# Attention stages with heads of 8 dimensions: halves of a batch half a slot apart, projections at a slot's end

## What is computed

```python
Q = (x @ Wq.T).reshape(B, xN, NUM_HEADS, HEAD_DIM)        # x: normalised rows
KV = (z @ Wkv.T).reshape(B, zN, 2, NUM_HEADS, HEAD_DIM)   # z: the context, 77 keys
attn = jnp.einsum('bqhd,bkhd->bhqk', Q, K) * SCALE
attn = jax.nn.softmax(attn, axis=-1)
O = jnp.einsum('bhqk,bkhd->bqhd', attn, V).reshape(B, xN, DIM)
return O @ Wo.T
```

## Time and profile before

| what | value |
|---|---|
| median of 3 runs | 6037.49 us (6032.2 to 6039.96) |
| the profiled execution, its own time | 6016.21 us |
| its span, first to last instruction | 6014.5 us |
| granted TensorE clock over the span | 0.916 of full speed |
| PE, PEld, DVE, ACT, POOL busy | 82%, 60%, 65%, 45%, 36% |
| first and last start of `score` in `l0x` | 41.2 and 636.4 us |
| first and last start of `score` in `l2x` | 2583.4 and 3181.3 us |

### The profile page before, as it was taken

One profiled execution on the slowest core, in us unless ns is written; L12 is line 12 of the kernel. 1 busy time (PEld: TensorE's weight loads), 2 busy tenths in 40 slices (PEclk: granted clock), 3 DMA queues, 4 the chain that ended last, 5 costly groups with the idle time before them and its releaser, 6 DMA issues. The chain is left out here.

```text
span 6014.5 us, 133734 instructions
## 1 busy us (share of the span) xinstructions
PE 4935.3 (82%) x41787; PEld 3611.9 (60%) x41787; DVE 3921.6 (65%) x9897; ACT 2728.1 (45%) x5454; POOL 2172.3 (36%) x3095
## 2 busy tenths in 40 slices
PE   6888898999962798078888998888898799998888
PEld 3555466888862465045555665776776577776544
DVE  4555585777766333245555776888887688888544
ACT  3444475555530233044444554555554355554344
POOL 4333100111117100733332334777775733333300
PEclk9999798999985899579997998999999899999988
DMA  1000500000011333100000000000000000000000
GB/s 37 5 4 3 242 0 14 5 5 5 5 49 43 115 135 115 50 10 5 4 3 12 1 0 9 0 0 0 0 0 5 7 2 2 2 2 6 1 11 18
DMA packets 108942, 140.25 MB, mean 23 GB/s; under 512 B 35832, under 2 KB 83256, under 8 KB 103996
## 3 DMA queue, kind: packets, MB, share of 16 engines
q1 hardware_dynamic: 100544, 120.88, 6.0%
q0 software_dynamic: 8192, 16.79, 1.0%
HBM read 47.44 MB, written 58.72 MB: 18 GB/s over the span
## 5 line engine op out<-in xcount | busy, mean ns | idle before, releaser
L2170 POOL TENSOR_TENSOR l3a_probs<-l3a_probs,l3a_later 128x512 f32<-128x512 f32 x256 | 320.7, 1281 | 4.9 <-DVE l3a_total L2358 4.9
L2156 POOL TENSOR_TENSOR l3a_keys<-l3a_kT,head 128x2048 f32<-128x2048 f32 x64 | 230.4, 3600 | 232.8 <-ACT l3a_kT L2283 232.8
L1585 POOL DMA_INDIRECT l1c_rows<-l_rows,l1f_slots x128 | 123.1, 961 | 442.5 <-PEq L1577 402.0
L2218 PE MATMUL l3a_scores<-l3a_keys,l3a_qT 128*128 128x512 f32 x512 | 255.1, 601 | 4.2 <-POOL l3a_keys L2156 4.2
L170 POOL TENSOR_TENSOR l1x_ve<-l1x_mv,eps 128x1 f32<-128x1 f32 x64 | 12.2, 190 | 657.6 <-DVE l1x_mv L162 657.6
L965 DVE SCALAR_TENSOR_TENSOR l0x_p_lo<-l0x_turned,l0x_p_hi 128x512 f16<-128x512 f32 (+1 forms) x192 | 115.7, 603 | 204.4 <-ACT l0x_p_hi L891 202.2
L298 PE MATMUL l3a_po<-l3a_vals,l3a_probsT 128*128 128x32 f32 x2048 | 248.0, 269 | 0.2
L965 DVE SCALAR_TENSOR_TENSOR l2x_p_lo<-l2x_turned,l2x_p_hi 128x512 f16<-128x512 f32 (+1 forms) x192 | 115.7, 603 | 202.8 <-ACT l2x_p_hi L891 200.6
L298 PEld LDWEIGHTS l3a_po<-l3a_vals,l3a_probsT 128*128 128x128 f32 x2048 | 246.8, 192 | 0.7 <-ACT l3a_probsT L279 0.4
L1656 POOL TENSOR_TENSOR l2f_hid<-l2f_prod,l2f_route 128x512 f32<-128x512 f32 x128 | 152.1, 1193 | 257.0 <-DVE l2f_prod L1803 253.7
L254 ACT ACTIVATE l3a_probs<-l3a_probs 128x512 f32<-128x512 f32 x256 | 161.7, 632 | 182.4 <-DVE l3a_probs L245 177.2
(11 more groups left out here) (581 smaller groups left out, 17374.6 us busy)
## 6 DMA issues: line engine op xcount, KB each, us to landing
l_rows<-l0f_zeros SPq DMA_DIRECT2D x34, 1024.0 KB, 26.2
l1f_parts<-l1f_split SPq DMA_DIRECT2D x40, 512.0 KB, 3.6
l1e_x_in<-l_rows SPq DMA_DIRECT2D x40, 256.0 KB, 2.8
l1f_down<-l1f_w SPq DMA_DIRECT2D x40, 256.0 KB, 2.3
l_rows<-l1e_y_out SPq DMA_DIRECT2D x40, 256.0 KB, 2.7
l1f_w<-in_L_W SPq DMA_DIRECT2D x16, 256.0 KB, 3.4
out_x<-x_res SPq DMA_DIRECT2D x16, 256.0 KB, 2.0
x_res<-in_x SPq DMA_DIRECT2D x1, 3840.0 KB, 12.2
```

The lines of the kernel that those rows point to most:

```text
L2156: pool.tensor_tensor(keys[it.par][:, :, :, :], kT[it.par][:, :, :].unsqueeze(2).to_broadcast([P, J, G4, T]), g.head32[:, :].unsqueeze(1).u ...
L2170: pool.tensor_tensor(v, v, later[:, :].unsqueeze(1).to_broadcast([P, 4, T]), ALU.mult).then_inc(s_masked, 1)
L2218: pe.matmul(scores[c][:, 0:G4 * T], qT[it.par][:, c, :], keys[it.par][:, c, :, :].rearrange("p h t -> p (h t)"), start=True, stop=True).th ...
```

## The change

In both stages, the order of all four compute engines is written anew, the softmax halves are set half a slot apart, and the three transposes of a batch are divided over two slots: `turn0` stands in the batch's own slot (`1 if u else 0`), `turn1`, `turn2`, all of `weigh`, `divide`, `turn_o`, `output` and `add` in the slot behind it (`ago` 1 where it was 2 for the last four). Of the front, `x`, `norm`, `rest` (of the context) and `c` move to an earlier turn (lag 0), and PE's `q`, `k`, `v0` and `x` stand at the end of slots 0, 1, 2 and 3, `v1` in the middle of slot 3. A piece's `blank` matmul stays in units 0 and 1 and goes from unit 2 (one of nine). `make_attention_constants` moves from `init` to the start of POOL's list in `l0x`. POOL waits for other counts in `context_rest`.

```diff
@@ pool, l0x and l2x
+                if first_use:
+                    make_attention_constants(pool, g, g.s_made)
...
-                    if (due := nth(it, 8, 3, ago=1)) is not None:
+                    if (due := nth(it, 4, 0, ago=1)) is not None:
+                        pool.wait_ge(s_keys, due)
+                    if (due := nth(it, 8, 7, ago=2)) is not None:
                         pool.wait_ge(s_ml, due)
...
-                skewed(pool, n, slots(steps, ["maxA value1 maxB s1", "maxA maxB rest s2 " + ("bias" if biased else ""),
-                                              "maxA maxB deviation s3", "maxA maxB next value0"]), 6)
+                skewed(pool, n, slots(steps, ["maxA s1 maxB value0", "maxA deviation s2 maxB value1",
+                                              "maxA s3 maxB " + ("bias" if biased else ""), "maxA next maxB rest"]), 6)
@@ tensor
-                        if c < 9:
+                        if u < 2:
...
-                         "turn_o": (turn_o, 2, 2), "output": (output, 2, 2)}
+                         "turn_o": (turn_o, 2, 1), "output": (output, 2, 1)}
...
-                    steps[f"turn{u}"] = (lambda it, j, u=u: turn(it, j, u), 2, 1)
+                    steps[f"turn{u}"] = (lambda it, j, u=u: turn(it, j, u), 2, 1 if u else 0)
...
-                fronts = ["v1 x", "q", "k", "v0"]
-                skewed(pe, n, slots(steps, ["scoreA turn0 turn_o scoreB output " + f + " mtA turn1 weigh0 shiftA mtB turn2 shiftB weigh1 weigh2"
-                                            for f in fronts]), 6)
+                fronts = [("", "q"), ("", "k"), ("", "v0"), ("v1", "x")]
+                skewed(pe, n, slots(steps, ["scoreA turn1 turn2 weigh0 mtA weigh1 shiftA weigh2 scoreB turn0 " + mid +
+                                            " turn_o mtB output shiftB " + end for mid, end in fronts]), 6)
@@ scalar
-                fronts = ["v1 x", "c q", "k", "v0"]
-                skewed(act, n, slots(steps, ["o high0 " + f + " mA high1 expA mB high2 expB" for f in fronts]), 6)
+                fronts = [("x", "v0"), ("q", "v1"), ("k", ""), ("", "c")]
+                skewed(act, n, slots(steps, [begin + " high1 high2 mA expA " + mid + " high0 o mB expB" for begin, mid in fronts]), 6)
@@ vector
-                fronts = ["norm v1", "q", "k stats", "v0"]
-                skewed(dve, n, slots(steps, ["divide maxA rest0 maxB add " + f + " rest1 rest2" for f in fronts]), 6)
+                fronts = [("", "", "stats"), ("q", "", "norm"), ("k", "", ""), ("v0", "v1", "")]
+                skewed(dve, n, slots(steps, ["maxA rest1 rest2 " + begin + " maxB divide rest0 " + mid + " add " + end
+                                             for begin, mid, end in fronts]), 6)
@@ init, gpsimd
-                    make_attention_constants(pool, g, g.s_made)
```

More of the change, by code:

```diff
@@ L688, in _ @@
                 steps = {"maxA": (lambda it, j: split_max(it, j, 0), 2, 0), "maxB": (lambda it, j: split_max(it, j, 1), 2, 0)}
-                one = {"deviation": (lambda it, j: fr.inverse_deviation(pool, it), 0, 0), "rest": (lambda it, j: context_rest(it), 1, 0),
-                       "bias": (lambda it, j: add_bias(it), 1, 0), "value0": (lambda it, j: value_rest(it, 0), 1, 0),
+                one = {"deviation": (lambda it, j: fr.inverse_deviation(pool, it), 0, 0), "rest": (lambda it, j: context_rest(it), 0, 0),
+                       "bias": (lambda it, j: add_bias(it), 1, 0), "value0": (lambda it, j: value_rest(it, 0), 2, 0),
                        "value1": (lambda it, j: value_rest(it, 1), 2, 0), "next": (lambda it, j: spread(it, 0), 1, 0),
@@ L897, in fetch_o @@
                     act.copy(oT[j % 2][:, :], oT_p).then_inc(s_oT, 1)
[L899 removed]
+                steps = {"c": (lambda it, j: context_high(it), 0, 0), "x": (lambda it, j: fetch_x(it), 1, 0),
                          "q": (lambda it, j: fetch_q(it), 1, 0), "k": (lambda it, j: fetch_k(it), 1, 0),
[L901 removed]
+                         "v0": (lambda it, j: fetch_v(it, 0), 2, 0), "v1": (lambda it, j: fetch_v(it, 1), 2, 0), "o": (fetch_o, 2, 1)}
                 for h, half_name in enumerate("AB"):
@@ L905, in _ @@
                 for u in range(3):
-                    steps[f"high{u}"] = (lambda it, j, u=u: high(it, j, u), 2, 1)
-                fronts = ["v1 x", "c q", "k", "v0"]
-                skewed(act, n, slots(steps, ["o high0 " + f + " mA high1 expA mB high2 expB" for f in fronts]), 6)
+                    steps[f"high{u}"] = (lambda it, j, u=u: high(it, j, u), 2, 1 if u else 0)
+                fronts = [("x", "v0"), ("q", "v1"), ("k", ""), ("", "c")]
+                skewed(act, n, slots(steps, [begin + " high1 high2 mA expA " + mid + " high0 o mB expB" for begin, mid in fronts]), 6)
             @block.vector
@@ L985, in add @@
                     dve.scalar_tensor_tensor(x, y_p, g.gates[:, gate:gate + 1], x, ALU.mult, ALU.add).then_inc(s_x, 1)
-                steps = {"stats": (lambda it, j: statistics(it), 0, 0), "norm": (lambda it, j: fr.normalize(dve, it), 1, 0),
+                steps = {"stats": (lambda it, j: statistics(it), 0, 0), "norm": (lambda it, j: fr.normalize(dve, it), 0, 0),
                          "q": (lambda it, j: query_rest(it), 1, 0), "k": (lambda it, j: key_rest(it), 1, 0),
-                         "v0": (lambda it, j: block_values(it, 0), 1, 0), "v1": (lambda it, j: block_values(it, 1), 2, 0),
-                         "divide": (divide, 2, 2), "add": (add, 2, 2)}
+                         "v0": (lambda it, j: block_values(it, 0), 1, 0), "v1": (lambda it, j: block_values(it, 1), 1, 0),
+                         "divide": (divide, 2, 1), "add": (add, 2, 1)}
                 for h, half_name in enumerate("AB"):
@@ L993, in _ @@
                 for u in range(3):
-                    steps[f"rest{u}"] = (lambda it, j, u=u: rest(it, j, u), 2, 1)
-                fronts = ["norm v1", "q", "k stats", "v0"]
-                skewed(dve, n, slots(steps, ["divide maxA rest0 maxB add " + f + " rest1 rest2" for f in fronts]), 6)
+                    steps[f"rest{u}"] = (lambda it, j, u=u: rest(it, j, u), 2, 1 if u else 0)
+                fronts = [("", "", "stats"), ("q", "", "norm"), ("k", "", ""), ("v0", "v1", "")]
+                skewed(dve, n, slots(steps, ["maxA rest1 rest2 " + begin + " maxB divide rest0 " + mid + " add " + end
+                                             for begin, mid, end in fronts]), 6)
 def l0_ffn(nc, g, a):
```

4 lines of the change are left out of this document (2 added, 2 removed).

## The result

The changed kernel takes 6013.9 us (median of 6 runs, 6007.9 to 6027.6), the kernel before in the same comparison 6038.9 (6 runs): a ratio of 0.996, 95% interval 0.9945 to 0.9974. It is 25 us faster; 114 were forecast. The profiled execution took 6007.9 us, 8.4 less than that of before; the part of the program between the two attentions, which the change doesn't touch, took 15 us more in it, so it hides some of the gain. (In the trace of before the last `add` of `l0x` lies at 653.7 us and the first `norm` of `l2x` at 2570.1; after, they are at 649.6 and 2581.0.

The account below looks back on a forecast made before the run. A loop through all engines sets each slot, plus x's wait and a clock fall per group; 34.5 us groups win 50.0 + 52.4, start 3.3, ends 2 x 4: 114 us, giving 5924 us, range 5858 to 6025.

Parts of the forecast that it names:

- the count of low stretches: Both attentions: one to two 3.4 us spells at half clock per group of four slots, adding 2.0 us a group.
- the drain's 1.99: End of the stage before the change: PE busy 1.99 of 3.41 us, and the clock fell behind it.
- The price of a stretch: Each 3.4 us at half clock costs 1.3 us net of idle, 1.7 at most.
- The sign of being wrong that the prediction names: Clock under 0.9 over the attention stages, with falls in the slots of q and k.
- The slot at full clock: Attention slots at clock 1.00: 7.94 to 8.25 us each, 32.5 a group against 37.36 before.
- the vanished wait of `x`: PE's 2.5 us wait for DVE's v_f before x was to drop under 0.6 us.
- Start and ends: Earlier start from moving the constants wins 3.3 us once; shorter stage ends win 4 us in each attention.
- (d): Most given back: 2.5 to 4 low-clock stretches, 35.8 to 37.7 us a group, 5965 to 6026 us; chance 0.13.
- the range for eight in ten: Total time forecast between 5858 and 6025 us.
- (c): Clock falls in every slot: 4.5 to 6 low stretches a group, 6048 to 6108 us; chance 0.13.
- (b): An engine round trip 0.3 us longer than read in every slot: 38 us, total 5962; chance 0.14.
- (a): Clock holds throughout both attentions: 32.5 us a group, 63 us below the forecast, 5861; chance 0.14.

Follow-up runs that it names:

- the run with 16 columns: Changed kernel plus, per slot, five matmuls on zeros before turn_o (not in v1's slot) and two before output, each cut from 308 to 16 columns: 6002.5 us.
- the order with two waits in each slot: Kernel before with x moved to the end of its slot behind v1, v1 copied out ahead of norm, and value1 behind the second maximum: 5925.9 us.
- the run with five and two zero matmuls: Changed kernel plus 308-column matmuls adding zeros: five before turn_o in slots without v1, two before output in every slot; 5893.3 us, no falls.
- 46 in another order: Changed kernel with divide before B's maximum and o before high0 except in v1's slot, five zero-adding matmuls before mtB there, two before every output: 5874.0 us.

## Why the prediction was wrong

**The step that failed** is the count of low stretches, "I take one to two a group, as one comes in each group now": there are 3.4 and 2.8, and in the kernel before it was not one but 1.4 and 1.6, since a fall can last two stretches or three. The reason behind it was that PE busy 2.4 of 3.4 us lies nearer to the ordinary slots, 2.83, than to the drain's 1.99. The second half came out as read (2.51 and 2.55), and it fell. The busy share was the wrong thing to compare: a stretch of before with 2.33 us busy held, and one with 2.75 fell in the run with 16 columns (rows above). What the runs show is that columns put into the thin half hold the clock, and the same instructions without columns don't. The ordinary slots of before have `weigh` spread over three places, with blanks near every wait, whereas the new order puts all of it into the first half; that this is why the order of before holds is in keeping with the runs, but none moved `weigh` by itself. The price of a stretch, 1.3 us, was right. 3.1 instead of 1.5, by 1.3 us and 31.5 groups: 66 us. The sign of being wrong that the prediction names, a clock under 0.9 over these stages with falls in the slots of q and k, came: 0.85 and 0.86.

**The slot at full clock** was 33.1 a group instead of 32.5, 19 us. (By the run without falls, 33.3, it is 25 us, and the clock's share 58 instead of 66; the sum is the same.) The steps hold up to `turn_o` (6.04 instead of 5.95 behind `scoreA`); the front begins at 7.38 instead of 7.23, q then lasts 0.1 longer than I read, and the slot with v1 and x has the 8.15 forecast. The waits, their order and sizes, and the vanished wait of `x` (0.8 once) are as forecast.

**Start and ends.** I counted 3.3 won at the start; the constants' move did win 2.4, but the order of the fronts, which I costed at nothing, puts 2.9 us in front of the first `score`, and again 3.0 in `l2x`. The ends gave 1.0 and 4.0 instead of 4 each. Together 10 us. With 66 and 19 it makes 95, and 93.5 are missing: slots 3.6 + 15.4, ends 5.0, less starts 3.5, are 20.5 us gained in place of 114.

**The rivals.** It is (d), most given back: 3.1 stretches lie in its 2.5 to 4, and 6014 in its 5965 to 6026. So the range for eight in ten held the time, but only by the part of (d) that it took in. Its mechanism and that of (c) are one, and (c) was decided against only by the count, 4.3. By the Trainium skill ("TensorE: Matmul & The Clock Gate", "A second HAM failure mode: psum-queue depth-cycling") short idles between groups of matmuls, frequent enough, make the clock oscillate; the trace agrees, with 58 falls and no wait over 0.7 us that recurs in every group. By that rule alone the order with two waits in each slot, up to 0.9 us and more in all (`x` at the slot's end), should fall too; it fell 3 times. (b), a longer round trip, is there in the 0.6 a group and no more. (a), the clock that holds, is what the run with five and two zero matmuls brought about, at 5893.3.

## What to carry to other kernels

Before balancing waits over slots, look at what TensorE streams around each of them: one long wait a group brought half as many falls as a short one or two in each slot's thin half, and two short waits a slot with work around them brought hardly any. Where a wait must stay, work of many columns ahead of it that changes no result is worth trying; here it took 2% off at next to no cost in the slots. Then look at the instruction queue, since what is put into a loop's body can make its turns slow. And mend the one long wait first: moving `x`, and what hangs on it, won four times what the new order did.

## What the runs showed of the hardware

**Code of a loop.** At some lengths and places of the loop's code PE stood still for 2.7 to 4.7 us at a turn of the loop, with 9 packets of 16.4 KB on the instruction queue for each stop; 30 matmuls of 16 columns more in the loop's body brought eight stops (6073.5 us). With 46 more matmuls there was one stop (all of 16 columns, 6002.5 us) or none (30 of 308 columns and 16 of 16, 5896.4 us; all of 308 columns, 5893.3 us). With 46 in another order there were two (5874.0 us). The Trainium skill ("Runtime: NRT & Kernel Launch", "Instruction fetch mechanics") says that a taken branch whose target isn't held any more forces a fetch before execution can go on; the packets agree. Which lengths and places do it stays open.

**DVE held by POOL.** At the start of either attention four TENSOR_SCALARs of 128x128 took 2.68 us on DVE, 1.12 before, one of them 1.91, while a TENSOR_TENSOR of POOL ran for 1.87 us beside them (rows of the start, above). In the order of before, POOL's came later. By the Trainium skill ("SBUF — State Buffer", "SBUF: two separate sides") the two engines share one pair of ports, held for a whole instruction; the durations are in keeping with it. No run here moved one of them alone, so the cause is only argued. With the constants back in `init` the four took 2.67 us again, beside 1.96 us of POOL's. It costs 1.6 us at each start, half of what the new order loses there.
